# Moving PSUM evictions between ScalarE and VectorE in a transformer layer, with a second pair of statistics buffers

## The reference

```python
Q = relu(x @ wq.T) / s;  K = relu(x @ wk.T) / s;  V = x @ wv.T;  U = silu(x @ wu.T)
KV = einsum('bhld,bhle->bhde', K, V);  O = einsum('bhld,bhde->bhle', Q, KV)
x1 = layernorm(x + (srms_norm(O) * U) @ wo.T)

logits = l2norm(x1) @ l2norm(sim_matrix, 0) - sigmoid(gates)
w = softmax(masked relu(logits)) * mask                    # 16 experts per token
q, k, v = [einsum('ne,neh->nh', w, einsum('nc,ech->neh', x1, p)) for p in (q_proj, k_proj, v_proj)]
ao = softmax(causal(q @ k.T / sqrt(128))) @ v
x2 = layernorm(x1 + einsum('enh,ehc->nc', einsum('ne,nh->enh', w, ao), o_proj))
```

## Time and profile before

| | us |
|---|---|
| median of the runs (2 runs, 8069.78 to 8104.02) | 8086.9 |
| the profiled execution | 7424.59 |
| its span, first to last instruction, slowest core | 7423.1 |
| spans of the eight cores | 7404.4 to 7423.1 |
| TensorE busy (matmuls) | 5245.0 (71%) |
| VectorE busy | 2349.1 (32%) |
| ScalarE busy | 1173.6 (16%) |
| mean granted TensorE clock, share of full speed | 0.826 |
| phase2c, about | 2610 to 4150 |
| phase3b, about | 5600 to 6115 |

### The profile page before, as it was taken

One profiled execution on the slowest core, in us unless ns is written; L12 is line 12 of the kernel. 1 busy time (PEld: TensorE's weight loads), 2 busy tenths in 40 slices (PEclk: granted clock), 3 DMA queues, 4 the chain that ended last, 5 costly groups with the idle time before them and its releaser, 6 DMA issues.

```text
span 7423.1 us, 62525 instructions; the slowest of 8 cores (7404.4 to 7423.1 us)
## 1 busy us (share of the span) xinstructions
PE 5245.0 (71%) x23902; PEld 2410.3 (32%) x24274; DVE 2349.1 (32%) x2353; ACT 1173.6 (16%) x1254; POOL 378.8 (5%) x534
## 2 busy tenths in 40 slices
PE   2999993997777755555556399999992446656655
PEld 1444441442222211111111144444441224434433
DVE  0000000002222224444343345444445543333333
ACT  0111110113333311111111000000003321111111
POOL 0000000000000010000000000000000000000000
PEclk9999996997777777777777699999995557777777
DMA  7010107334212121111113533535310001111111
GB/s 115 12 23 12 23 1 126 78 74 97 63 46 57 46 68 57 57 57 57 57 57 77 91 40 37 83 39 81 40 23 0 1 3 49 51 49 57 52 51 54
DMA packets 284967, 382.37 MB, mean 52 GB/s; under 512 B 13555, under 2 KB 226676, under 8 KB 284164
## 3 DMA queue, kind: packets, MB, share of 16 engines
q0 software_dynamic: 197536, 277.38, 20.2%
q1 hardware_dynamic: 87140, 100.97, 4.0%
HBM read 453.81 MB, written 100.66 MB: 75 GB/s over the span
## 4 chain that ended last, share of the span: by engine, by line
PE 66%; DVE 17%; ACT 7%; issue 4%; another core or an unknown queue 4%; DMA 1%; DVEq 1%; ACTq 0%; POOL 0%; PEldq 0%; SPq 0%; POOLq 0%
PE pPE L1196 18%; PE pP L371 12%; PE pO L1511 8%; PE pU L566 6%; PE pW L790 6%; PE pQ L463 6%; DVE oarena L106 5%; ACT L106 3%; DVE vtm L106 2%; PE pR L869 2%; DVE kfm L106 2%; DVE Ssb L106 1%; ACT vtm L106 1%; DVE oust L106 1%
## 5 line engine op out<-in xcount | busy, mean ns | idle before, releaser
L106 ACT ACT_TABLE_LOAD x307 | 393.9, 1283 | 5044.0 <-DVE negm L106 1653.8
L1196 PE MATMUL pPE<-arena,ybf 128*128 128x512 bf16 x2635 | 581.6, 380 | 75.6 <-DMA ybf<-y_s 72.9
L1511 PE MATMUL pO<-qfm,oarena 128*128 128x256 bf16 x4096 | 599.3, 307 | 1.0 <-DVE qfm L106 1.0
L790 PE MATMUL pW<-aosb,arena 128*128 128x512 bf16 x1372 | 412.3, 464 | 230.2 <-DVE oarena L106 203.1
L463 PE MATMUL pQ<-xbf2a,arena 128*128 128x512 bf16 x2007 | 442.6, 380 | 127.4 <-DMA xbf2a<-x_fm 125.1
L566 PE MATMUL pU<-xbf2b,warena 128*128 128x512 bf16 x2000 | 475.6, 400 | 28.2 <-DVE oust L106 18.9
L1511 PEld LDWEIGHTS pO<-qfm,oarena 128*128 128x128 bf16 x4096 | 420.9, 109 | 161.8 <-issue 56.0
L371 PE MATMUL pP<-arena,xbf 128*128 128x512 bf16 x1999 | 445.8, 380 | 35.8 <-DMA xbf<-x_fm 33.3
L106 DVE TENSOR_TENSOR uf<-ofp,uf 128x512 f32<-128x512 f32 x128 | 88.6, 692 | 1193.0 <-ACT ofp L106 1193.0
L106 DVE TENSOR_TENSOR wstage<-pPE,wrt 128x1024 bf16<-128x1024 f32 x192 | 235.1, 1224 | 727.2 <-PE pPE L1196 716.8
L371 PE MATMUL pP<-warena,xbf 128*128 128x512 bf16 x2006 | 445.0, 379 | 2.2
(11 more groups left out here) (169 smaller groups left out, 4654.3 us busy)
## 6 DMA issues: line engine op xcount, KB each, us to landing
xs<-x_fm POOLq DMA_DIRECT2D x128, 256.0 KB, 4.5
y_s<-oarena SPq DMA_DIRECT2D x32, 1024.0 KB, 11.4
ybf<-y_s POOLq DMA_DIRECT2D x32, 1024.0 KB, 10.4
vtm<-y_s POOLq DMA_DIRECT2D x128, 256.0 KB, 3.1
z_fm<-a SPq DMA_DIRECT2D x64, 512.0 KB, 5.1
xbf<-x_fm POOLq DMA_DIRECT2D x32, 512.0 KB, 9.5
xbf2a<-x_fm POOLq DMA_DIRECT2D x32, 512.0 KB, 12.8
qbf_s<-qst SPq DMA_DIRECT2D x32, 512.0 KB, 4.0
```

Source lines behind the costliest of these rows:

```text
L106: ins = attr(*a, **k)
L790: ins = e.matmul(pW[:, i, :], arena0[:, j, s * 128:(s + 1) * 128], ouv(slot)[:, j - 4 * qf, :], start=(j == 4 * qf), stop=(j == 4 * qf + 3))
L1196: ins = e.matmul(pPE[:, g % 2, nn * 512:(nn + 1) * 512], ybv(gc)[:, j, tau * 128:(tau + 1) * 128], wsrc[:, j, nn * 512:(nn + 1) * 512], st ...
L1511: ins = e.matmul(pO2[:, s % 4, 0:T], oarena[:, ei, s * 128:(s + 1) * 128], waoF[:, ei, :], start=(ei == 0), stop=(ei == E - 1))
```

## The change

In phase2c a second pair of buffers, `asq4b` and `ab4bb`, is allocated. The groups `sg` = 0 and 2 use the old pair, 1 and 3 the new pair, and `ssg(sg)` waits for `tsgm(sg - 2)` (for `sg` < 2: for `tsgm(t - 1, sg + 2)`). The eviction of `pW` in quarter 0, `sg > 0`, is a `tensor_copy` on VectorE in place of the activation on ScalarE. In phase3b the evictions of score blocks are split: VectorE takes the blocks 0, 2, 4, 6 of a strip, and a new ScalarE function `sSs`, emitted between VectorE's and the mask, takes the blocks 1, 3, 5, 7 by an activation Copy with scale. TensorE waits for the engine that holds the slot.

```diff
             with nc.sbuf_tensor("xs", [128, 6, 2, T], F32) as xs, \
+                 nc.sbuf_tensor("asq4b", [128, 4, T], BF16) as asq4b, \
+                 nc.sbuf_tensor("ab4bb", [128, 4, T], BF16) as ab4bb, \
...
-                    if qf == 0 and sg > 0:
-                        def vag_s(e, t=t, sg=sg, ab4=ab4):
-                            C1.wait(e, M[("tg", t, 0, sg)])
-                            if t >= 2:
-                                SM.wait_mark(e, M[("ystore", t - 2)])
-                                C1.wait(e, M[("tsgm", t - 2, 3)])
-                            e.activation(ab4, pW[:, :, :], AF.Copy)
-                        Se(vag_s)
-                        M[("va", t, qf, sg)] = (C2, C2.n)
...
+                        pW4 = pW[:, :, :]
+                        if qf == 0:
+                            if sg == 0:
                                 e.tensor_tensor(ab4, pW4, xs4(t, 0), ALU.add)
                             else:
+                                e.tensor_copy(ab4, pW4)
+                        else:
+                            e.tensor_tensor(ab4, ab4, pW4, ALU.add)
+                            if sg == qf:
+                                e.tensor_tensor(ab4, ab4, xs4(t, qf),
+                                                ALU.add)
+                    Ve(vag)
+                    M[("va", t, qf, sg)] = (C3, C3.n)
...
+                        asq4 = asq4a if sg % 2 == 0 else asq4b[:, :, :]
+                        ab4b = ab4ba if sg % 2 == 0 else ab4bb[:, :, :]
+
+                        def ssg(e, t=t, sg=sg, asq4=asq4, ab4b=ab4b):
                             cwait(e, M[("va", t, 3, sg)])
-                            if sg > 0:
-                                C1.wait(e, M[("tsgm", t, sg - 1)])
+                            if sg >= 2:
+                                C1.wait(e, M[("tsgm", t, sg - 2)])
                             elif t > 0:
-                                C1.wait(e, M[("tsgm", t - 1, 3)])
+                                C1.wait(e, M[("tsgm", t - 1, sg + 2)])
...
-                                if kb >= 2:
-                                    C3.wait(e, b3c + kb - 1)
+                            if kb >= 2:
+                                kp = kb - 2
+                                if kp % 2 == 0:
+                                    C3.wait(e, b3c + kp // 2 + 1)
                                 else:
-                                    C3.wait(e, sevpos[g - 3])
+                                    C2.wait(e, b2c + (kp - 1) // 2 + 1)
+                            elif g > 2:
+                                cwait(e, sevd[g - 2])
...
-                        for kb in range(nkb):
+                        for kb in range(0, nkb, 2):
                             g = gk0 + kb + 1
                             C5.wait(e, b5 + g)
                             N = min(512, Lk - kb * 512)
                             e.tensor_scalar(Ssb[:, kb * 512:kb * 512 + N],
                                             pS[:, g % 2, 0:N],
                                             ISC, None, ALU.mult)
-                            sevpos.append(C3.n)
-                    Ve(sS)
+                            sevd[g] = (C3, C3.n)
+                    Ve(sSv)
+
+                    def sSs(e, i=i, Lk=Lk, nkb=nkb, gk0=gk0):
+                        for kb in range(1, nkb, 2):
+                            g = gk0 + kb + 1
+                            C5.wait(e, b5 + g)
+                            N = min(512, Lk - kb * 512)
+                            e.activation(Ssb[:, kb * 512:kb * 512 + N],
+                                         pS[:, g % 2, 0:N],
+                                         AF.Copy, scale=ISC)
+                            sevd[g] = (C2, C2.n)
+                    Se(sSs)
```

More of the change, by code:

```diff
@@ L716, in phase2c @@
             rsq = vtv[0:1, 512:1024]
-            ab4b = vtm[:].rearrange("p a b -> p (a b)")[:, 2048:4096] \
+            ab4ba = vtm[:].rearrange("p a b -> p (a b)")[:, 2048:4096] \
                 .rearrange("p (a b) -> p a b", a=4)
-            asq4 = qfm[:, 0:2048].rearrange("p (a b) -> p a b", a=4)
+            asq4a = qfm[:, 0:2048].rearrange("p (a b) -> p a b", a=4)
             _ou01 = aosb[:].rearrange("p a b -> p (a b)") \
@@ new lines, in vag @@
+                    def vag(e, t=t, qf=qf, sg=sg, ab4=ab4):
+                        C1.wait(e, M[("tg", t, qf, sg)])
+                        if qf == 0 and t >= 2:
+                            SM.wait_mark(e, M[("ystore", t - 2)])
+                            if sg == 0:
+                                C1.wait(e, M[("tsgm", t - 2, 3)])
+                        if sg == qf:
+                            for pg in (2 * qf, 2 * qf + 1):
+                                SD.wait_mark(e, M[("xp", t, pg, 0)])
+                                SD.wait_mark(e, M[("xp", t, pg, 1)])
+                        pW4 = pW[:, :, :]
+                        if qf == 0:
+                            if sg == 0:
@@ L831, in emit_stats @@
+                    Ve(vag)
+                    M[("va", t, qf, sg)] = (C3, C3.n)
                 def emit_stats(t, sg):
                     if True:
-                        def ssg(e, t=t, sg=sg):
+                        asq4 = asq4a if sg % 2 == 0 else asq4b[:, :, :]
+                        ab4b = ab4ba if sg % 2 == 0 else ab4bb[:, :, :]
+                        def ssg(e, t=t, sg=sg, asq4=asq4, ab4b=ab4b):
                             cwait(e, M[("va", t, 3, sg)])
-                            if sg > 0:
-                                C1.wait(e, M[("tsgm", t, sg - 1)])
+                            if sg >= 2:
+                                C1.wait(e, M[("tsgm", t, sg - 2)])
@@ L837, in ssg @@
                             elif t > 0:
-                                C1.wait(e, M[("tsgm", t - 1, 3)])
-                            e.activation(asq4[:, :, :],
+                                C1.wait(e, M[("tsgm", t - 1, sg + 2)])
+                            e.activation(asq4,
                                          abuf[:, t % 2, 4 * sg:4 * sg + 4, :],
                                          AF.Square)
-                            e.activation(ab4b[:, :, :],
+                            e.activation(ab4b,
@@ L1291, in phase3b @@
                 gkb = [0]
-                sevpos = []
+                sevd = {}
                 def emit_strip_front(i):
@@ L1297, in emit_strip_front, with tS @@
                     gk0 = gkb[0]
-                    def tS(e, i=i, Lk=Lk, nkb=nkb, gk0=gk0):
-                        b3c = C3.n
+                    b3c, b2c = C3.n, C2.n
+                    def tS(e, i=i, Lk=Lk, nkb=nkb, gk0=gk0,
+                           b3c=b3c, b2c=b2c):
                         for kb in range(nkb):
                             g = gk0 + kb + 1
-                            if g > 2:
-                                if kb >= 2:
-                                    C3.wait(e, b3c + kb - 1)
-                                else:
-                                    C3.wait(e, sevpos[g - 3])
+                            if kb >= 2:
+                                kp = kb - 2
+                                if kp % 2 == 0:
+                                    C3.wait(e, b3c + kp // 2 + 1)
+                                else:
+                                    C2.wait(e, b2c + (kp - 1) // 2 + 1)
+                            elif g > 2:
+                                cwait(e, sevd[g - 2])
                             N = min(512, Lk - kb * 512)
@@ L1315, in emit_strip_front, with sSv @@
                     gkb[0] += nkb
-                    def sS(e, i=i, Lk=Lk, nkb=nkb, gk0=gk0):
+                    def sSv(e, i=i, Lk=Lk, nkb=nkb, gk0=gk0):
                         if i > 0:
                             C2.wait(e, M[("exp", i - 1)])
-                        for kb in range(nkb):
+                        for kb in range(0, nkb, 2):
                             g = gk0 + kb + 1
```

## The result

| | before, us | after, us |
|---|---|---|
| the profiled execution | 7424.59 | 7207.58 |
| shortest of the runs | 7427.13 | 7193.29 |
| median of all runs | 7930.13 (10 runs) | 7374.66 (11 runs) |
| ratio, after to before (undisturbed runs) | | 0.9693, 95% interval 0.9668 to 0.9718 |

The change makes the kernel 3.1% faster. The medians of all runs are further apart, because in many runs of either kernel some cores have a lower clock for a while and the slowest core then sets the time; only the undisturbed runs are compared, and that is what the ratio does. The forecast of 7887 us lay 512 us above the measured median, and even its lower end, 7800, was too high. In the profiled execution the step forecast was 7199; 7207.6 was measured.

The account below looks back on a forecast made before the run. In phase2c's quarter 0 TensorE and ScalarE were taken to alternate, waiting on each other. Profile: 7424.6 - 262 (phase2c) + 36 (phase3b) = 7199 us; median: 8087 - 200 = 7887 us, range 7800 to 7945.

Parts of the forecast that it names:

- Turns in quarter 0: Phase2c: a turn of projection and statistics matmuls falls from 20.23 to 8.88 us; 21 turns gain 238 us.
- the rival in which the clock stays down: Phase2c, quarter 0: the clock does not rise, gain only 170 us, time 7917 or 7968 us; chance 0.10.
- Chunk 0: Phase2c's first chunk, without statistics: evictions get shorter, but VectorE waits for the load of xs; gain counted as 0.
- Tail: End of phase2c: with two buffers the last chunk's four statistics groups follow sooner; gain 24 us.
- Phase3b: Attention strips: 28 added table loads and waits for slots make strips 4 to 31 longer; 36 us lost.
- the upper bound: Phase3b: 87 us lost if each of the 68 score activations on ScalarE had a table load.
- part 2: Phase3b: every second score block goes to ScalarE; 36 us lost, about 0 if copy needs no load.
- Sum for the profiled execution: Whole kernel: 7424.6 less 262 from phase2c plus 36 from phase3b gives 7199 us, 226 less.
- the last one, from the profiled execution to the time of the runs: Whole kernel: 200 us taken off the median of 8087 gives 7887 us.
- 662 us: Whole kernel: measured median above the profile, assumed to come from long dense stages slowed by up to 25%.
- 51 us: Phase2c: gain lost if the newly gapless turns and tail are slowed like the dense stages, leaving 175 us.
- The slower rival: Phase3a: denser phase2c pulls its clock down; at 0.80 it costs 300 us, net 74 slower, 8161; chance 0.04.

Follow-up runs that it names:

- e4: The whole change, with phase3b's exp, aosb copy and ScalarE score evictions merged into one ScalarE function; shortest time 7150 us, ratio 0.9547.
- e5: The whole change, with phase3b's three ScalarE functions merged into one and pS given four slots instead of two; shortest time 7113 us, ratio 0.9498.
- e10: The kernel before with only the phase2c edits, plus four slots of pS (VectorE takes all score blocks); shortest time 7166 us, phase3b 462.7 us.
- e9: The whole change with four slots of pS, functions not merged; phase3b 470.6 us, shortest time 7370 us (four cores lost some 200 us in other stages).
- e3: The whole change, with each score eviction on ScalarE in phase3b a function of its own; shortest time 7250 us, phase3b 541.1 us.

## Why the prediction was right in its steps and wrong in its time

- **Turns in quarter 0**: right. Forecast 8.88 us a turn and 34 a chunk, measured 8.81 and 34.1 (a chunk 153.6 us instead of 187.7). All 24 waits for vtm of the earlier trace rows are gone but one of 0.44 us in the tail, and the granted clock over the three turns is 1.00. Some 9 us of a turn's gain are the gap and the rest is the clock; so the rival in which the clock stays down falls.
- **Chunk 0**: I counted 0, because of the wait for xs. On core 0, from the first W to the first S of chunk 1, it took 134.8 us before and 130.0 after, 5 us less. This is what makes phase2c 268 us shorter and not 262. My reading of rows 7 was wrong: the row names the load as what came last, but the matmuls of the group that the add takes out had ended only 0.45 us before it (2663.14). In the kernel after, the same row names xs again, the matmuls end 0.45 us before the add again, and the add starts 45.4 us behind the first W (2628.31) instead of 50.1 (2613.53). So the load did not hold the chunk in place. The matmuls of the group before, then the matmuls and the add of the group after:

```profile
2657.84 5.30 PE L790 MATMUL pW<-aosb,arena 128*128 128x512 bf16 x16 [2.61 <-DVE oarena L106]
```

```profile
2669.70 3.61 PE L792 MATMUL pW<-aosb,arena 128*128 128x512 bf16 x16 [2.61 <-DVE oarena L106]
...
2673.76 2.29 DVE L106 TENSOR_TENSOR oarena<-oarena,pW 128x2048 f32<-128x2048 f32 x1 [4.21 <-DMA xs<-x_fm]
```

- **Tail**: 24 us forecast, 24.2 measured.
- **Phase3b**: 36 us forecast, 34.5 measured (core 0), with a load for each emitted ScalarE function (311, as said). The count of 68 blocks in the upper bound should have been 64. The page "ScalarE: Activation LUTs" of the Trainium skill, section on table sets, says that copy is in every set. e4 agrees (Exp, then Copy, without a load between), and the trace of after does not contradict that statement, but shows that a load comes all the same at the head of each function. What I took from the page, that part 2 would cost nothing, does not follow from it. The other page of the Trainium skill, "TensorEngine Tiling (Array Packing)", section on the PSUM bottleneck, says to use both engines for evacuation. The trace of e5 against e10 agrees, with 46 us for split and merging together on four slots; with two slots they brought 12 (e4), and with the load ahead of the split it cost 8 (e9) or 35 (the change).
- **Sum for the profiled execution**: 7199 forecast, 7207.6 measured, on different slowest cores, so that the closeness is in part luck. The cores of the kernel after start phase2c at 2600 to 2628 us, and the slowest core moved from 0, which started at 2613.5 before, to 1, which starts at 2628.3: 15 us that the change has nothing to do with, against the 5 us of chunk 0 that I had not counted.
- **The step that failed is the last one, from the profiled execution to the time of the runs.** I added 662 us to it because two runs lay at 8070 and 8104, and took that for a fixed part of the kernel's time, which the changed kernel would show too. It is none. In later rounds the kernel before also took 7427 to 7448 us, within 0.3% of its profile, and on a chip where one die lost hundreds of us the other was at 7420. The change takes 217 us (profiled executions) to 234 us (shortest runs) off that floor; I had forecast 226 there and 200 for the runs. Two runs cannot say how often a long one comes, and the profile, 8% below both, should have been a centre of its own: the range had to reach to 7200, or to be given as two ranges.
- **The guess about where the 662 us lie was right in the main, what I made of it was wrong.** The two runs of 8070 and 8104 us have no trace. In the three executions that have one, such losses lie mostly in the dense stages, phase1, phase2a and phase3a, and for a smaller part in phase2b and phase3c. But I took 51 us off the gain in the same way, and half of that went into the 200, as if the newly gapless turns would be slowed likewise. No execution shows that: phase2c was as long on slowed cores as on others. The page "TensorE: Matmul & The Clock Gate" (Part 1) of the Trainium skill speaks of a limit of 13/16 for a die on which three cores run dense matmuls. The 0.81 in the pieces of 20 us above is that level, and the windows of 0.88 and 0.90 are means of it and 1.00. Yet all eight cores run these stages in each execution and most show 1.00, and cores 4 and 5 of e9 lost time in phase3a while 6 and 7 of the same die did not. So the trace agrees with the page on the level and, in the main, on the stages, but not on when it happens, nor on its holding the whole die; what sets it off and what releases it stays open.
- **The slower rival**, that a denser phase2c pulls the clock of phase3a down, falls: the clock is 0.98 and the stage 1352 us long in both profiled executions.

## What to carry to other kernels

Look at what stands ahead of a slow helper step in its engine's order, not only at its buffers: a second buffer was worth nothing until the eviction ahead of it had gone to another engine. A split of evictions over two engines wants more slots than engines (with two slots 12 of the 47 us came), and no table load at the head of the added function; count functions of ScalarE as well as instructions. And before the time of a kernel on all cores is forecast, its profile is to be held against the shortest run, not the median of two: where they differ by per cents, forecast the step on the profile's level, and give the runs a range that reaches there.

## What the runs showed of the hardware that was not expected

- Exp, Copy and Copy of another tensor ran under one table load (252 loads in e4), while Copy behind Copy had a load of 1.28 us when a new ScalarE function began (e3, 1.21 us each on the chain).
- The granted clock of a slowed core is not a little lower throughout: in pieces of 20 us it stood at 0.81 for hundreds of us, or went between 0.81 and 1.00, with TensorE as busy as at 1.00. Within one execution pairs of cores of one die lost time in different stages: cores 4 and 5 of e9 142 us in phase3a, cores 6 and 7 some 200 us ahead of phase2c, while phase3b was the same on all eight cores to 0.6 us.
- ScalarE and VectorE took blocks out of PSUM side by side at full pace: 0.60 and 0.69 us in e5, against 0.60 for ScalarE alone and 0.69 for VectorE alone.
